# The second sort's histogram counted by two digits of the block number

## The reference

```python
def reference(x, src, dst, edge_type_33, edge_weight1, ...):
    edge_index = jnp.stack([src, dst])
    x = _layernorm(x + _L0_gnn_ref(x, L0_gnn_relation_emb, edge_index, edge_type_33))  # sums at src
    x = _layernorm(x + _L1_gnn_ref(x, edge_index, edge_weight1, ...))                  # sums at src
    x = _layernorm(x + _L2_gnn_ref(x, edge_index, ...))                                # sums at dst
    x = _layernorm(x + _L3_gnn_ref(x, edge_index, ...))                                # sums at dst
    return x
```

## Time and profile before

| | |
|---|---|
| median of three runs | 30460.42 us |
| the profiled execution, its own time | 30229.77 us |
| its span | 30228.0 us |
| busy in the span: GpSimd, TensorE, VectorE | 54%, 39%, 29% |
| granted TensorE clock, mean | 0.517 of full speed |
| sort 0, from the first scatter to the last | 97.4 to 2838.9 us |
| sort 1, first scatter | 2855.0 us |

### The profile page before, as it was taken

One profiled execution on the slowest core, in us unless ns is written; L12 is line 12 of the kernel. 1 busy time (PEld: TensorE's weight loads), 2 busy tenths in 40 slices (PEclk: granted clock), 3 DMA queues, 4 the chain that ended last, 5 costly groups with the idle time before them and its releaser, 6 DMA issues. The chain is left out here.

```text
span 30228.0 us, 205466 instructions
## 1 busy us (share of the span) xinstructions
PE 11768.9 (39%) x50455; PEld 9840.4 (33%) x50456; DVE 8821.3 (29%) x14192; ACT 2073.6 (7%) x3825; POOL 16385.0 (54%) x16724
## 2 busy tenths in 40 slices
PE   2222222245555555554555533333333333333333
PEld 1001111134444444444455422332232222223222
DVE  4334333335555455553111211121111112111111
ACT  0000000012222222221000000000000000000000
POOL 5555444445555355554555466556656665665665
PEclk5555555555555555555555555555555555555555
DMA  0000111222222222221101111111111111111111
GB/s 19 1 1 19 38 40 40 71 74 71 68 72 70 62 71 71 69 72 39 20 19 20 21 23 23 22 23 23 23 23 23 23 23 25 23 23 23 23 23 25
DMA packets 803024, 1093.34 MB, mean 36 GB/s; under 512 B 449066, under 2 KB 529390, under 8 KB 742884
## 3 DMA queue, kind: packets, MB, share of 16 engines
q0 software_dynamic: 528384, 511.86, 8.7%
q1 hardware_dynamic: 274404, 579.20, 5.5%
HBM read 877.63 MB, written 212.42 MB: 36 GB/s over the span
## 5 line engine op out<-in xcount | busy, mean ns | idle before, releaser
L528 POOL DMA_INDIRECT rows<-table_lin,pay x9984 | 9444.5, 946 | 6821.1 <-issue 3866.0
L777 PE MATMUL pair<-rows,onehot 128*128 128x64 f32 x19968 | 4790.2, 422 | 765.6 <-issue 765.6
L777 PEld LDWEIGHTS pair<-rows,onehot 128*128 128x128 f32 x19968 | 4502.7, 331 | 1289.0 <-issue 1288.7
L1632 DVE TENSOR_TENSOR acc<-acc,pair 128x1024 f32 x832 | 1016.1, 1221 | 13196.2 <-remote 11852.0
L765 PE MATMUL pair<-ones_bf,zeros_bf 1*128 1x512 bf16 x1664 | 837.5, 604 | 8874.0 <-issue 8859.5
L528 POOL DMA_INDIRECT rows<-table_hyp,pay x3328 | 3432.3, 1031 | 1143.0 <-issue 984.3
L765 PEld LDWEIGHTS pair<-ones_bf,zeros_bf 1*128 1x128 bf16 x1664 | 109.3, 99 | 9002.8 <-issue 9002.8
L739 PE MATMUL pair<-tab,sel_t 128*128 x6656 | 1687.8, 435 | 2976.2 <-ACT sel_t L980 2411.3
L512 POOL DMA_INDIRECT payload_dst<-rows x1600 | 1560.8, 975 | 1906.0 <-DVEq L1286 1430.9
L739 PEld LDWEIGHTS pair<-tab,sel_t 128*128 128x128 f32 x6656 | 1480.3, 327 | 3289.8 <-issue 3289.8
L512 POOL DMA_INDIRECT payload_src<-rows x1600 | 1555.1, 972 | 1284.3 <-DVEq L1286 711.9
(11 more groups left out here) (319 smaller groups left out, 14991.1 us busy)
## 6 DMA issues: line engine op xcount, KB each, us to landing
onehot<-head_hots SPq DMA_DIRECT2D x208, 1024.0 KB
rows<-table_lin,pay POOLq DMA_INDIRECT x9984
rel<-rel_rows SPq DMA_DIRECT2D x52, 1072.0 KB
xs<-rel_rows SPq DMA_DIRECT2D x52, 1072.0 KB
head_hots<-msg SPq DMA_DIRECT2D x52, 1024.0 KB
head_hots<-onehot SPq DMA_DIRECT2D x52, 1024.0 KB
rows<-table_hyp,pay POOLq DMA_INDIRECT x3328
rel_rows<-rel SPq DMA_DIRECT2D x26, 1072.0 KB
```

What stands on the lines that cost most here:

```text
L528: pool.indirect_dma_start(out=rows[:, h, t, 0:width], out_offset=None, in_=table[:, :], in_offset=bass.IndirectOffsetOnAxis(ap=pay[:, h, t ...
L777: last = nc.tensor.matmul(sums[:, bass.ds(at, D)], onehot[:, h, t, :], mv, start=False, stop=False, skip_group_check=True)
L1632: V.tensor_tensor(flat_acc[:, at], flat_acc[:, at], ps_half[u], ALU.add)
```

## The change

Sort 1's histogram is made by two digits as well. Inside sort 0's loop VectorE makes two small one-hots in the place of `later`, 40 columns of 13 and of 8 values, and TensorE multiplies them five columns at a time (eight matmuls of 65 by 40, each with its own weights) into the bank that sort 0's digit counts used. `starts` now does the same two closing steps for both sorts: the diagonal on VectorE, and the sum over partitions on TensorE (`total`). The digits of the second key are made once, ahead of `starts(0)`, by the four operations that made those of the first (`make_digits`).

```diff
-        later = flat_hot.bitcast(BF16)[0:EP, 2 * HC * NB:4 * HC * NB].rearrange("p (h c b) -> p h c b", h=2, b=NB)
+        later = flat_hot.bitcast(BF16)[0:EP, 2 * HC * NB:2 * HC * (NB + HI + LO)].rearrange("p (h n) -> p h n", h=2)
+        later_hi = later[:, :, 0:HC * HI].rearrange("p h (c v) -> p h c v", v=HI)
+        later_lo = later[:, :, HC * HI:HC * (HI + LO)].rearrange("p h (c v) -> p h c v", v=LO)
...
-            def count(k, hot_, h, first):
-                for c in range(NCH):
-                    last = nc.tensor.matmul(ps_total[k][:, 0:CH * NB], ones_bf[0:EP, :],
-                                            hot_[:, h, c * CH:c * CH + CH, :].rearrange("p c b -> p (c b)"),
+            def count_digits(hi, lo, h, first, done):
+                columns = hi.shape[2]
+                for c in range(0, columns, CH):
+                    last = nc.tensor.matmul(ps_digits, hi[:, h, c:c + CH, :].rearrange("p c v -> p (c v)"),
+                                            lo[:, h, c:c + CH, :].rearrange("p c v -> p (c v)"),
                                             start=first and c == 0, stop=False, skip_group_check=True)
-                last.then_inc(S["hist_counted", k], 1)
+                last.then_inc(done, 1)
+
+            def total(k):
+
+                pe.wait_ge(classes_ready, k + 1)
+                nc.tensor.matmul(ps_total[k][:, 0:CH * NB], ones_f, by_class.rearrange("p (c b) -> p c b", c=CH)[:, :, 0:NB],
+                                 start=True, stop=True).then_inc(S["hist_counted", k], 1)
...
                 for h in range(2):
                     rank(0, i, h)
                     degrees(0, i, h, False)
                     await_reg(pe, "pe", S["count_hot", 1], 2 * i + (h + 1))
-                    count(1, later, h, False)
-
+                    count_digits(later_hi, later_lo, h, False, S["hist_counted", 1])
+
+            total(1)
             place_from_start(1)
...
             def starts(k):
 
-                if k == 0:
-                    dve.wait_ge(S["hist_counted", 0], PARTS)
-                    V.tensor_tensor(by_class.rearrange("p (c v w) -> p c v w", c=CH, v=HI),
...
-                dve.wait_ge(S["hist_counted", k], 2 * GITERS if k else PARTS + 1)
+                counted = 2 * GITERS if k else PARTS
+                dve.wait_ge(S["hist_counted", k], counted)
+                V.tensor_tensor(by_class.rearrange("p (c v w) -> p c v w", c=CH, v=HI),
...
+                dve.drain().then_inc(classes_ready, 1)
+                dve.wait_ge(S["hist_counted", k], counted + 1)
...
+            def digit_hots(hi, lo, h, cols, n):
+
+                for o, key, v in ((hi, hi_key, HI), (lo, lo_key, LO)):
+                    V.tensor_tensor(o[:, h, :, :], over(key[:, cols], v),
+                                    ps_sort_iota[0:EP, 0:v].unsqueeze(1).to_broadcast([EP, n, v]), ALU.is_equal)
...
             make_key(1)
+            make_digits(1)
 
             starts(0)
...
                     await_reg(dve, "dve", S["hist_counted", 1], 2 * i + (h - 1))
-                    make_hist(1, later, h, i * (2 * HC) + h * HC)
+                    digit_hots(later_hi, later_lo, h, bass.ds(i * (2 * HC) + h * HC, HC), HC)
                     dve.drain().then_inc(S["count_hot", 1], 1)
             starts(1)
```

More of the change, by code:

```diff
@@ L673, in _ @@
                 pe.wait_ge(S["count_hot", 0], part + 1)
-                for c in range(0, PC, CH):
-                    last = nc.tensor.matmul(ps_digits, hi_hot[:, part % 2, c:c + CH, :].rearrange("p c v -> p (c v)"),
-                                            lo_hot[:, part % 2, c:c + CH, :].rearrange("p c v -> p (c v)"),
-                                            start=part + c == 0, stop=False, skip_group_check=True)
-                last.then_inc(S["hist_counted", 0], 1)
-            pe.wait_ge(classes_ready, 1)
-            nc.tensor.matmul(ps_total[0][:, 0:CH * NB], ones_f, by_class.rearrange("p (c b) -> p c b", c=CH)[:, :, 0:NB],
-                             start=True, stop=True).then_inc(S["hist_counted", 0], 1)
+                count_digits(hi_hot, lo_hot, part % 2, part == 0, S["hist_counted", 0])
+            total(0)
             place_from_start(0)
@@ L687, in _ @@
                 pe.wait_ge(S["count_hot", 1], h + 1)
-                count(1, later, h, h == 0)
+                count_digits(later_hi, later_lo, h, h == 0, S["hist_counted", 1])
             with pe.Fori(1, GITERS) as i:
@@ L1324, in _ @@
                 rank(0, 0, h)
-                make_hist(1, later, h, h * HC)
+                digit_hots(later_hi, later_lo, h, bass.ds(h * HC, HC), HC)
                 dve.drain().then_inc(S["count_hot", 1], 1)
```

36 lines of the change are left out of this document (17 added, 19 removed).

## The result

The changed kernel takes 30539.43 us (median of 9 runs, 30519.51 to 30573.11) against 30458.12 of the kernel before on the same chip (9 runs, 30432.69 to 30472.88): ratio 1.0029, interval 1.0019 to 1.0039. It is about 81 us slower, where 228 us less were forecast.

A forecast was written before the change was run, and what follows sets the result against it. It took a ring of waits in sort 0, with TensorE slowed while GpSimd scatters, as the bound. Terms -228 (38 halves x 6.0), +4.2 and -4 were summed to -228, so 30460.4 gives 30232 us, range 30070 to 30380.

The forecast's parts named there:

- The ring: Sort 0's loop: engines wait on each other in turn, none near full; at most 711.9 us to win.
- The window: Sort 0, until about 54.5 us after GpSimd's start: TensorE slow, picks inside cost nothing, later ones 2.01 us each.
- the half that the prediction worked out: Sort 0's loop: first pick at 30.6 us, five picks in the window, half 63.8 us, 6.0 less.
- The price of the count in the window: TensorE in sort 0: by columns, eight old matmuls cost 19.6 us a half, eight small ones 2.5.
- rival 4: Sort 0's loop: small pairs with new weights cost over 2.45 us each, so slower, 30575 us; chance 0.04.
- VectorE's smaller work at nothing: Sort 0's loop: VectorE loses 4.24 us, gains 0.56 + 0.35 a half; costed at nothing, hidden by TensorE's queue.
- Ahead of sort 0, 4.2 us: Before sort 0: making the second key's digits on VectorE adds 4.2 us straight on the path.
- Between the sorts: From sort 0's end to sort 1: smaller count against new diagonal and sum matmul, 4 us less.
- Rival 1: Sort 0's loop: scatters, not TensorE, hold the pick back; half stays 69.8 us, time 30461; chance 0.12.
- Rival 3: Sort 0's loop: less TensorE work eases the slowing, 10 us a half, 380 less, 30080 us; chance 0.10.

The follow-up runs named there:

- e2: Kernel before, plus one unread 4.24 us VectorE operation between the picks and GpSimd's release in each half of sort 0: 30378.18 us, ratio 1.0055.
- e3: Kernel before, with both histograms counted by digits ahead of sort 0 and no count in its loop: 29941.37 us, ratio 0.9911.
- e17: Kernel before, with 8 scatters per half in sort 0 instead of 40, on a chip where TensorE is late: 28969.43 us, ratio 0.95.
- e14: Kernel before, with 8 scatters per half in sort 0 instead of 40, on a chip without lateness: 22099.2 us, ratio 0.9688.
- e5: e3 plus eight unread matmuls of 490 columns in the count's place in TensorE's queue: 30235.25 us, ratio 1.0006 to the kernel before.
- e4: e3 plus eight unread matmuls of 65 by 40, each with its own weights, in the count's place: 30231.65 us, ratio 1.0007 to the kernel before.
- e7: Kernel before, with a half's degrees and count queued on TensorE behind the next half's ranking rounds in sort 0: 30387.38 us, ratio 1.0058.
- e6: Changed kernel, with VectorE still making the old wide one-hot, unread: 30280.62 us, ratio 1.0021 to the kernel before.
- e1: Kernel before, unedited, profiled once more: 30161.11 us in one run, beside 30207.46.
- e18: Changed kernel, with its two small one-hots made behind the next half's wide one-hot: 30537.41 us, ratio 1.001 to the kernel before.
- e13: Changed kernel, run again on a chip without lateness: 22844.05 us, ratio 1.0013 to the kernel before.
- e19: Kernel before, with both histograms ahead of sort 0 and the degrees' one-hot made ahead of the picks in both sorts: 29969.55 us, ratio 0.9827.
- e8: Changed kernel, with a half's degrees and count queued on TensorE behind the next half's rounds: 30348.82 us, ratio 1.0043 to the kernel before.

## Why the prediction was wrong

**The ring is the bound: right.** e2 pays 170 us for 40 x 4.24, and e3 wins.

**The window: right.** Picks before some 54.5 us after GpSimd's start come 5.6 us apart and cost nothing, later ones 2.0. e3 is the half that the prediction worked out: it said first pick at 30.6, five in the window, half 63.8; with no count at all it is 26.9, 5.6 and 62.3. The slowing by scatters, inferred there from waits, is shown by e17, with 32.9 us a half for 8 scatters in sort 0 and 89 for 40 in sort 1 of the same trace. The lateness was found on A and B alone: on chip C, with the same 40 scatters, e14's sort 1 takes 51.6 us a half.

**The price of the count in the window: the step that failed.** It read "at 5.0 us per thousand the old ones cost 19.6 us" and took 2.5 for the eight small ones. The old ones were sized well (17.3 in e5). The small ones cost 18.9 (e4). The rate per column came from rounds of 490 columns, 5.0, and from one stretch of 40 narrow and 9 wide pairs, 5.13, which agreed. The trace of before holds the parts of that stretch: from the taking up to the degrees' increment 19.5 us, 0.49 a pair, and from there to the first pick 20.0 for nine pairs, 2.2 each. The first 36 or so narrow pairs are taken up at full speed (e7's rows) and what follows them is not, which made 0.87 us a pair look like an upper bound for narrow ones. The prediction had the right number as the far end of its bounds ("if a pair in the window costs the same whatever its width, 19.6, nothing gained") and as rival 4, to which it gave 0.04. Rival 4 named 2.45 us a pair as the point from which the change loses; 2.36 was measured (e4) against 2.16 for the wide ones (e5), a distance that the medians of e4 and e5 don't bear out. So this step explains why the 228 us were not won. It does not explain the 81 us lost.

**The sum with the measured terms.** e4 against e5 is 5 us in all by the medians; e6 against e1 is 2.0 us a half by the traces, 78 in 39 halves. So the loop gives 5 to 78 us. With 4.1 ahead of sort 0 and, between the sorts until sort 1's first scatter, 6.5 more by the two pages (4.4 by e6 against e1) instead of 4 less, the range is 14 to 89; 81 was measured. What lies between the two is not taken apart: e4's matmuls wait for no one-hot of their own, the change's do, and it is open why the kernel became slower and not merely no faster.

**VectorE's smaller work at nothing: no gain from it, as forecast**; VectorE stands 44.6 us idle in the half shown. Whether its two small operations are part of the loss no run takes apart (e6 and e18 above).

**Ahead of sort 0, 4.2 us: right** (101.5 against 97.4).

**Between the sorts the forecast had the sign wrong:** 4 less, and 4 to 7 more were measured. The new matmul and the diagonal are paid there, and no gain from the smaller count shows.

**Rival 1, the scatters hold the pick whatever the matmuls are, was wrong as put**: without count the pick comes 17 us earlier. **Rival 3, less work eases the slowing**, was wrong: eight pairs cost 17 to 19 us at either width.

**What stays open.** Which resource the scatters take from TensorE isn't shown. Their packets don't differ with the lateness: a half has 1280 of them, of some 17 ns each, in the traces of before, of after and of e13 alike; the first begins 1.55 us after GpSimd's start in the trace of before and 0.27 in e13, the last is done at 51.5 and 50.4. TensorE's records have "issue" there, and its granted clock is at or near the lower of its two levels with lateness and without: a mean of 0.57 in e3 and 0.51 in e13 between 200 and 1300 us. The clock isn't it. Why chips of one kind are free of it is open as well, and what the small one-hots add in the changed kernel beside e4.

## What to carry to other kernels

Where a trace shows TensorE late beside another engine's indirect transfers, price its instructions in that stretch by their number and not by their columns, until both widths have been measured there; a rate made from one width alone says nothing of the other. If work must leave such a stretch, take the instructions out (e3) or put them ahead of the release, where 40 pairs took 3.1 to 3.4 us (e19, sort 1), and look at what the next round of scatters then runs into (e7, e8, and e19 in sort 0). And where a kernel is to run on more than one chip, measure on more than one: the loop that decides all on one chip decided nothing on another.

## What was not expected of the hardware

- In the scatters' stretch a pair of weights and matmul takes 2.16 us with 490 columns and 2.36 with 40 (e5, e4), 2.80 in e7's rows, where outside it 64 small ones take 3.82 us.
- Waits in that stretch come in steps of 0.70 us, VectorE's before its picks too (e3, timeline of VectorE):
```profile
1799.65 0.67 DVE L1278 TENSOR_TENSOR rows<-pair,onehot 125x490 f32<-125x490 f32 x1 [4.19 <-remote]
...
1820.64 0.67 DVE L1278 TENSOR_TENSOR rows<-pair,onehot 125x490 f32<-125x490 f32 x1 [2.78 <-remote]
1822.66 0.67 DVE L1278 TENSOR_TENSOR rows<-pair,onehot 125x490 f32<-125x490 f32 x1 [0.59 <-PE pair L605]
...
1863.52 0.67 DVE L1278 TENSOR_TENSOR rows<-pair,onehot 125x490 f32<-125x490 f32 x1 [3.49 <-remote]
```
- The kernel before takes 30210, 30460 to 30500 and 22810 to 22840 us on different chips. It isn't only the sorts: in the passes behind them GpSimd's gathers (L530) wait 6855.5 us in the page of after and 3943.7 in e13, with the same busy time (groups of instructions, after and then e13):
```profile
L530 POOL DMA_INDIRECT rows<-table_lin,pay x9984 | 9468.0, 948 | 6855.5 <-issue 3863.2
```
```profile
L530 POOL DMA_INDIRECT rows<-table_lin,pay x9984 | 9469.2, 948 | 3943.7 <-issue 3908.1
```
